# A graph network's first edge pass: GpSimd waits for three of four gathers to land before it issues the next four

## The reference

```python
s_n, v_n = _equiv_layernorm(s, v, gamma_s, beta_s, gamma_v)
msg_s = (s_n @ Ws_src)[src] + (s_n @ Ws_dst)[dst]
msg_v = einsum('ncx,cd->ndx', v_n, Wv_src)[src] + einsum('ncx,cd->ndx', v_n, Wv_dst)[dst]
w1 = rbf @ W_rbf
m1_s, m1_v = _cg_tp(msg_s, msg_v, y0, y1, ...w1...)
a = leaky(m1_s @ W_alpha) . alpha_dot            # softmax over the edges of each target
val_s, val_v = m1_s @ Ws_val, einsum('ecx,cd->edx', m1_v, Wv_val)
val_v = val_v * sigmoid(val_s @ Wg)[..., None];  val_s = sigmoid(val_s)
m2_s, m2_v = _cg_tp(val_s, val_v, y0, y1, ...)
h = concat(m2_s @ Ws_vlin, einsum('ecx,cd->edx', m2_v, Wv_vlin))
agg = segment_sum(alpha * h, dst)                # then projection, residual, layer norm
```

## Time and profile before

| | us |
|---|---|
| median of 3 runs | 9591.08 |
| lowest, highest | 9548.35, 9623.26 |
| the profiled execution: its own time | 9599.6 |
| its span, first to last instruction | 9597.3 |
| granted TensorE clock, mean of the span | 0.836 |

### The profile page before, as it was taken

How to read it: one execution, slowest core, us unless ns; L and a number is a source line. 1 busy time by engine, 2 the same in 40 slices (tenths; PEclk the granted TensorE clock), 3 DMA queues, 4 the chain that set the end, 5 groups by cost and what they waited for, 6 DMA issues and landing times. The chain is left out here.

```text
span 9597.3 us, 196058 instructions
## 1 busy us (share of the span) xinstructions
PE 7798.3 (81%) x43972; PEld 6155.8 (64%) x43973; DVE 6800.5 (71%) x16742; ACT 5176.7 (54%) x16950; POOL 5019.7 (52%) x5222
## 2 busy tenths in 40 slices
PE   5788888888878888888888887898788887887778
PEld 3677777777767777767777776897444444444446
DVE  7667667767767666676677777787777776776677
ACT  5455555555545555555555554113666666666665
POOL 1555555555545555555555553784366665565650
PEclk7777777777777777787777878999899999999999
DMA  7333222222222222222222222677444443443435
GB/s 242 74 77 76 78 75 77 77 77 78 78 68 78 77 75 75 76 79 75 74 78 78 77 76 59 220 223 153 116 113 114 111 112 104 110 112 107 111 105 174
DMA packets 971876, 968.06 MB, mean 101 GB/s; under 512 B 452750, under 2 KB 788750, under 8 KB 971662
## 3 DMA queue, kind: packets, MB, share of 16 engines
q0 software_dynamic: 225792, 385.65, 16.4%
q1 hardware_dynamic: 512032, 346.40, 13.0%
q10 hardware_dynamic: 233936, 234.90, 7.4%
HBM read 677.57 MB, written 288.65 MB: 101 GB/s over the span
## 5 line engine op out<-in xcount | busy, mean ns | idle before, releaser
L745 POOL DMA_INDIRECT e_g_dst<-table_dst,e_idx x1568 | 1495.5, 954 | 1695.2 <-ACT logits L898 1324.1
L784 PE MATMUL e_ps_t<-ident,e_m 128*128 128x128 f32 (+1 forms) x7840 | 1499.7, 334 | 687.0 <-issue 307.2
L745 POOL DMA_INDIRECT e_g_src<-table_src,e_idx x1568 | 1497.4, 955 | 988.6 <-issue 608.2
L2021 POOL DMA_INDIRECT f_e<-table,f_src x1568 | 1492.0, 952 | 980.8 <-issue 521.8
L784 PEld LDWEIGHTS e_ps_t<-ident,e_m 128*128 128x128 f32 (+1 forms) x7840 | 1128.0, 170 | 891.6 <-issue 598.8
L2078 PE MATMUL f_ps_a<-sums 128*128 128x384 f32 x3936 | 1514.7, 531 | 1.5 <-DVE sums L2178 1.5
L877 ACT ACTIVATE e_m1t<-e_ps_t 128x512 f32<-128x512 f32 (+1 forms) x1176 | 688.0, 598 | 950.2 <-remote 393.6
L2078 PEld LDWEIGHTS f_ps_a<-sums 128*128 128x128 f32 x3936 | 763.3, 204 | 569.7 <-issue 216.7
L2067 PE MATMUL f_ps_w<-f_w,f_hidden 64*128 64x192 f32 x3936 | 491.9, 372 | 494.1 <-DVE sums L2178 242.3
L1004 DVE TENSOR_TENSOR e_vy<-e_msg,e_ps_w 128x384 f32<-128x384 f32 x392 | 216.7, 553 | 817.4 <-ACT e_ps_w L957 513.2
L896 ACT ACTIVATE e_ps_v<-e_ps_v 128x128 f32<-128x128 f32 x392 | 102.7, 262 | 1284.4 <-remote 726.7
(11 more groups left out here) (268 smaller groups left out, 17900.8 us busy)
## 6 DMA issues: line engine op xcount, KB each, us to landing
edge_values<-e_h ACTq DMA_DIRECT2D x392, 330.0 KB
r_h<-edge_values SPq DMA_DIRECT2D x196, 660.0 KB, 4.0
sums<-sums ACTq DMA_DIRECT2D x492, 192.0 KB
e_g_src<-table_src,e_idx POOLq DMA_INDIRECT x1568
e_g_dst<-table_dst,e_idx POOLq DMA_INDIRECT x1568
f_e<-table,f_src POOLq DMA_INDIRECT x1568
f_rbf<-basis SPq DMA_DIRECT2D x492, 48.0 KB
basis<-t_part SPq DMA_DIRECT2D x42, 448.0 KB, 3.1
```

Source lines behind the costliest of these rows:

```text
L745: pool.indirect_dma_start(out=into[:, r, t, :], out_offset=None, in_=table, in_offset=bass.IndirectOffsetOnAxis(ap=idx[:, r, c:c + 1], axi ...
L784: last = nc.tensor.transpose(ps_t[bank][0:channels, t * P:(t + 1) * P], rows(t), ident[:])
L2021: pool.indirect_dma_start(out=rows_of_units[:, (place * RING + r) * T + t, :], out_offset=None, in_=table, in_offset=bass.IndirectOffsetOn ...
```

## The change

The four source gathers, the four target gathers and the fourth gather of each run get semaphores of their own. Before each run GpSimd waits until the first three gathers of the run ahead have landed (48 of the run's semaphore). DVE, before the messages of a unit, and SP, before it overwrites the unit's row numbers, wait on all three semaphores in place of one. No gather, buffer or operation of another engine is added or taken away, and the second edge pass stays as it is.

```diff
-        idx_in, y_in, rbf_in, gathered = (...)
+        idx_in, y_in, rbf_in, from_src, from_dst, fourths = (...)
...
             def load(u, r, i):
...
-                    wait(sp, gathered[r], i * 32 * T)
+                    wait(sp, from_src[r], i * 16 * (T - 1))
+                    sp.sem_inc(issued, 1)
+                    wait(sp, from_dst[r], i * 16 * (T - 1))
+                    sp.sem_inc(issued, 1)
+                    wait(sp, fourths[r], i * 32)
                     sp.dma_start(idx[:, r, :], idx_d[u]).then_inc(idx_in[r], 16)
...
                 wait(pool, first, (u - RING) * FIRST + MSG if not isinstance(u, int) or u >= RING else 0)
+                if not isinstance(u, int) or u > 0:
+                    pool.wait_ge(from_dst[(r - 1) % RING], (i + 1 if r else i) * 16 * (T - 1))
                 pool.sem_inc(issued, 1)
...
                     if side == 1 and (not isinstance(u, int) or u >= RING):
                         wait(pool, gated, u - RING)
+                    if side == 1:
+                        pool.wait_ge(from_src[r], (i + 1) * 16 * (T - 1))
                         pool.sem_inc(issued, 1)
                     for t in range(T):
...
-                        ).then_inc(gathered[r], 16)
+                        ).then_inc(landed[r] if t < T - 1 else fourths[r], 16)
...
             def message(u, r, i):
-                dve.wait_ge(gathered[r], (i + 1) * 32 * T)
+                dve.wait_ge(from_src[r], (i + 1) * 16 * (T - 1))
+                dve.wait_ge(from_dst[r], (i + 1) * 16 * (T - 1))
+                dve.wait_ge(fourths[r], (i + 1) * 32)
```

More of the change, by code:

```diff
@@ L625, in edges @@
                                                     sem("ones_set"))
-        idx_in, y_in, rbf_in, gathered = ([sem(f"{n}{r}") for r in range(RING)]
-                                          for n in ("idx_in", "y_in", "rbf_in", "gathered"))
+        idx_in, y_in, rbf_in, from_src, from_dst, fourths = ([sem(f"{n}{r}") for r in range(RING)]
+                                          for n in ("idx_in", "y_in", "rbf_in", "from_src", "from_dst", "fourths"))
         stored = [sem(f"stored{r}") for r in range(2)]
@@ L737, in gather @@
                 wait(pool, first, (u - RING) * FIRST + MSG if not isinstance(u, int) or u >= RING else 0)
+                if not isinstance(u, int) or u > 0:
+                    pool.wait_ge(from_dst[(r - 1) % RING], (i + 1 if r else i) * 16 * (T - 1))
                 pool.sem_inc(issued, 1)
-                for side, (table, into) in enumerate(((table_src, g_src), (table_dst, g_dst))):
+                for side, (table, into, landed) in enumerate(((table_src, g_src, from_src),
+                                                              (table_dst, g_dst, from_dst))):
                     if side == 1 and (not isinstance(u, int) or u >= RING):
                         wait(pool, gated, u - RING)
+                    if side == 1:
+                        pool.wait_ge(from_src[r], (i + 1) * 16 * (T - 1))
                         pool.sem_inc(issued, 1)
```

## The result

The changed kernel takes 9268.64 us (median of three runs, 9260.3 to 9270.94) against 9591.08 before: a ratio of 0.9665, 95% interval 0.9604 to 0.9727. Later comparisons give the change another sign altogether, as the experiments show. A comparison here is a set of runs of a changed kernel and of the kernel before, taken together. First this one.

What follows compares the result with a forecast made beforehand. The prediction took GpSimd's gathers as off the critical path, held back by ACT and DVE, with stops behind closely spaced gathers. 9600 - 212 (stops) + 5 (semaphores) = 9393, 8 lower against the median: 9385 us, range 9310 to 9640.

Steps and rivals of the forecast that it cites:

- Steps (1) and (2): GpSimd's waits ahead of target and source runs, first pass: gaps 1.1 to 1.3 and 1.2 to 2.0 us, cost 0.
- Step (3): DVE ahead of `e_msg` and SP ahead of loads wait on three semaphores instead of one: 5 us cost.
- Step (4): First pass: 35 DVE waits over 5.5 us before `e_vy`, 265 us in all; four fifths gone, 212 us saved.
- A: Rival, first pass: 1.2 us gaps lie near the limit, half the stops stay, 9470 us; chance 0.16.
- B: Rival, first pass: short gaps follow from TensorE running ahead, spacing brings nothing, 9590 to 9620 us; 0.24 with the rule.
- The rule weighed there: Rival: DMA engines serve queues in turn, so dense gathers can't hold up others' transfers; about 9600 us; 0.24 with B.
- C: Rival, first pass: later source runs shorten gaps ahead of target runs, making new stops, 9700 to 10,000 us; chance 0.15.
- D: Rival, GpSimd's waits: the three gathers have already landed, so runs aren't spaced, 9560 to 9640 us; chance 0.03.
- The profile after: Expected signs: gaps at least 1.1 us, logits waiting under 1324, `e_vy` idle 500 to 600, first pass 5430 to 5520 us.

Runs made afterwards that it cites:

- held: A way of running, not a kernel change: comparisons in which the unchanged kernel before takes 9591 to 10,045 us.
- quick: A way of running, not a kernel change: comparisons in which the unchanged kernel before takes 7807 to 7811 us; the changed kernel takes 8762.28 against 7810.46 us in one.
- second held comparison: The changed kernel measured again against the kernel before: 9754.02 us against 10,045.02, ratio 0.9695.
- the gap by work: Kernel before with three small GpSimd memsets behind each run of four gathers, no landing wait: 0.9346 (9371.64 us) where before takes 10,009.33, 1.1504 where it takes 7808.19.

## Why the prediction was right or wrong

**What bounds the kernel.** "GpSimd is thus held back by the others and not they by it" holds for the held execution that I had the earlier trace rows and for no quick one, where GpSimd bounds every unit at 10.2 us. I had the number for it in hand: a cycle of 9.4 us plus gaps, "11.8 to 13.9", which I found hidden under 14.5 us a unit. That the 14.5 us were themselves a disturbance, nothing but the "remote" rows could have told me.

**Steps (1) and (2), cost 0.** The sizes were right: least gaps of 1.12 and some 1.0 us against 1.1 to 1.3, and 1.34 us in the median ahead of source runs against 1.2 to 2.0. The cost of 0 was right in the held comparisons, covered by the waiting for logits, of which 808 us are left. In quick ones there is no cover: 2.41 us a unit, 12% of the kernel. That is the path which I had wrong beyond the result.

**Step (3), semaphores, 5 us.** 0.9999 [0.9989, 1.0009]: nothing, in a quick comparison; in a held one it wasn't measured.

**Step (4), the stops.** This is the step that missed, in two places. "Four fifths gone, since the gap is smaller than an ordinary one" was the wrong share: all 35 went. And the sum had nothing for units without a stop. Even with all stops gone it came to 9340 us, against 9271 for the profiled execution. The first pass gave 294 us against my 212 less 5, which makes 87 of the 116 us between 9385 and the result; most of the rest are the 35 us outside the pass. The 87 divide like this. From the twentieth unit on, loops of four units without a long wait take 55.4 us in the changed kernel and 56.0 in the one before, 0.6 x 98 = some 58 us over the pass, and that leaves some 236 for the stops, between my 212 and my 265. The 0.6 us are 1% and come from one trace of each kernel, so their size is rough; less late signals, 1.65 us against 2.3, fit with them. The limit that I looked for between 0.8 and 2 us lies at 0.95 to 1.05 us, and gaps of 1.1 us clear it nearly always. In the second held comparison the changed kernel has 15 waits over 5.5 us, but none over 6.5, where those of the kernel before mostly take 8 to 10.5; the share of stops gone there stays open, since the kernel before has no trace of that comparison.

**The cause.** I wrote that the engines stop "with nothing to wait for" and quoted the row of ACT's copy released by "remote" as one of them. They waited for TensorE's signals. What I took for the cause, two short gaps in a row, is the condition under which a hold outlasts a run, and not a cause by itself: quick executions have 0.3 us at every gap and no stop. So the direction was right on a mechanism that was half right, and right only because the result's comparison was a held one.

**The rivals.** A, half of the stops stay: not in the result. B, the short gap is a symptom: refuted in held comparisons by the gap by work, 0.9346 with the pauses of GpSimd left as they were; that something other than the gathers must be there as well is right. The rule weighed there, of the Trainium skill, "DMA: Bandwidth & Descriptors", "Queues, rings and completion order", stands: it speaks of transfers sharing the DMA engines, and what is held here are TensorE's signals. I was wrong to read from it that spacing the gathers would bring nothing. C, slower by new stops: no. The kernel can be slower, by another mechanism that I didn't list: gaps on an engine that turns out to be the bound. D: no.

**The profile after.** Gaps, the new row of waits, less waiting for logits, 528 us before `e_vy` (500 to 600), fewer than ten long waits (0) and 5440 us for the pass (5430 to 5520) came as said; the second pass moved by 25 us.

**What stays open.** What holds TensorE's signals in some comparisons and not in others, whether its work is held or only the signal, and why they come 1 us after the last gather. It isn't that this gather has landed: its recorded landings come 1.5 us after its end in the median, in held and quick traces alike, and so some 0.4 us behind the burst of late signals at 0.9 to 1.3 us. Not tried is whether the same time without gathers does as well inside a run; not known is what GpSimd's own pause is.

## What to carry to other kernels

Waits that the profile ends by "remote" on readers of TensorE's output mean that its signals come later than its record says: compare signal times with record times before calling an idle engine one with nothing to wait for. An engine that waits for others is off the critical path only in the way of running that was profiled; work out its own cycle beside the others' (9.4 us plus gaps here), and name what a wait costs if that becomes the bound. Have both kernels timed in more than one comparison: here the same change makes the kernel 3% faster or 12% slower. And look whether an edit moves a pause that it wasn't meant to touch.

## What the runs showed of the hardware

The same program takes 7.81 ms or 9.6 to 10.0 ms, steady within a comparison: every kernel's runs lie within 1.4% of each other. In the kernel before the signs of the second way begin with the first dense gathers and not only on TensorE. SP's timeline in the kernel before, held and then quick, at the start of the first pass:

```profile
246.90 0.01 SPq L720 DMA_DIRECT2D e_idx<-idx  x1
249.74 4.93 SPq L249 DMA_DIRECT2D e_rbf<-basis  x3
257.49 0.69 SPq L720 DMA_DIRECT2D e_idx<-idx  x1
```

```profile
243.67 0.36 SPq L720 DMA_DIRECT2D e_idx<-idx  x1
244.29 1.25 SPq L249 DMA_DIRECT2D e_rbf<-basis  x3
245.74 0.35 SPq L720 DMA_DIRECT2D e_idx<-idx  x1
```

Three loads take SP 4.93 us in one and 1.25 us in the other. Between 247 and 274 us of the held trace SP's register and issuing instructions start 0.70 or 1.40 us apart (once 2.1), in the quick one mostly 0.06 to 0.6. The second unit then takes 32.1 us in the held trace and 11.3 in the quick one, and the granted clock never settles at full speed, which it does from 262 us on in the quick one. The changed kernel's held trace, whose gathers are spaced, has few such steps there, and its second unit takes 11.6 us. Gathers themselves are alike in both ways of running, 0.95 to 0.97 us each.

Held traces also lack more of their semaphore events. The kernel before has 3167 of 3920 signals of TensorE and 15,645 of the 50,176 steps by which its gathers' landings raise semaphores; in the quick trace it has 3845 and 47,147.
